# Score pairs behind the values in a fused decoder kernel's attention

## The chip, the cores and the metric

The kernel runs on one core of one Trainium2 chip. The metric is the device time of one execution in microseconds (us). Each core has five engines with their own instruction streams: TensorE (PE, with its weight loads as PEld), VectorE (DVE), ScalarE (ACT), GpSimd (POOL) and SyncE (SP, which issues the transfers here). They meet only through semaphores.

## The reference, cut to what matters

One input of 2048 tokens by 128 channels passes six layers. The fifth, attention with 16 heads of 64 channels, is the one that matters here:

```python
xn = rms_norm(x, gamma)
qkv = xn @ w_qkv                     # 16 heads, 64 channels each
sim = einsum('bhid,bhjd->bhij', q * 64 ** -0.5, k)
attn = softmax(sim, axis=-1)
out = einsum('bhij,bhjd->bhid', attn, v)
x = x + out.reshape(b, n, 1024) @ w_out
```

A softmax needs the largest score of every query first. Before attention come a mixture of experts, a recurrent layer, a second mixture and a gated layer; after it a last gated layer. Those are not touched.

## The kernel before, in words

**Tiles.** Activations lie transposed, 128 channels by 2048 tokens. A head is worked through in four chunks c of 512 queries (`NC`, `CH`), and a chunk in eight groups g of two key tiles of 128 (`GROUPS`). I write (c,g). Precision comes from splitting: a value is an upper part (rounded) plus a lower part (the rest), and products are summed over the parts that matter.

**What TensorE does in a group** (`main_chunk`, line 941, in the tensor block), all matmuls with 512 columns:

- `scores_t` (line 879, matmuls at L890 and L891): the transposed scores of this head, two key tiles, four matmuls into two of four PSUM banks. It waits for ScalarE to be done with the group two before.
- `score_pair` (line 859, L868): two matmuls for the *next* head, 128 queries by 1024 keys, into banks 4 and 5. Only the maxima are taken from them. There is one such buffer, so each pair waits on `s_max` for the maximum of the pair before. `PAIRS_OF_MAXIMA` says how many pairs a group has: none in (0,0), two in (0,7), one in each other: 32 a head.
- `values` (line 894, L905 and L908): the probabilities of the group three before (`PV_LAG`) by V, four matmuls. It waits for the upper part from ScalarE and the lower part from POOL.
- then what the plan `SPARE` places into the one spare bank (6 or 7): turned maxima (L876), column sums (`column_sums`, L917), output product of an earlier chunk (`project_out`, L924), V of the next pair of heads (`project_v`, L854 to L856), Q and K two heads ahead (`project_qk`, L713 to L715). In chunk 3 the plan has the projection n=0 in (3,3), column sums in (3,4), projection n=1 in (3,5), output in (3,6), projection n=2 in (3,7). Before each of these, `evicted` (line 926) makes TensorE wait until the one before has been taken out of the bank. For a projection that is until both ScalarE (`hi_done`) and VectorE (`lo_done`) are done.

**What VectorE does in a group** (`main_chunk`, line 1626), in this order: a piece of the row sums (`whole_sum` of the chunk before, L1588, in groups 0 to 3; `first_half_sum`, L1574, in groups 4 to 7), then, where due, `low_qk` (L1564, lower half of a projection, in (3,4) and (3,6) by `LOW_QK`, and in (0,0) and (0,2) of the next head), `add_out` (L1612, adds an output product to x: in group 0, and in (3,7)), `invert` (L1608), `maxima_end` (L1600), and last `maximum` (line 1591, L1594) for each pair of the group.

ScalarE makes two exponentials of a group's scores (L1267, L1270), and evicts. POOL makes the lower part of the probabilities (`low_part`, L609), scales outputs (L632) and, once a head, makes V's lower part (L615). All these orders are written out by hand and are the same in all heads, but for the first, the last, and that heads 14 and 15 project no Q and K two heads ahead.

Of the kernel before, what the change touches and what calls it, by code (L numbers as in the profile page):

```python
# [38 lines left out]
PAIRS_OF_MAXIMA = ((0, 1, 1, 1, 1, 1, 1, 2), (1,) * 8, (1,) * 8, (1,) * 8)  # L39
# [47 lines left out]
def macaron_kernel(nc, a, out, g_scratch, l_scratch, r_scratch):  # L87
    ctx = ExitStack()
    with ctx:
# [165 lines left out]
        def chunk(c):  # L255
            return ds(c * CH, CH)
# [5 lines left out]
        def spare_bank(c):  # L262

            return 6 + (c + 1) % 2

        def chunk_of(head, c):

            return NC * head + c

        def before(head, c, by):  # L270

            c -= by
            while c < 0:
                head, c = head - 1, c + NC
            return head, c

        def exists(head):

            return not isinstance(head, int) or head >= 0

        def wait_hi_moved(eng, head, par, n):

            eng.wait_ge(hi_moved[par], 16 * MOVES_HI * (2 * (head - par) + n + 1))

        def wait_lo_moved(eng, head, par, n):

            eng.wait_ge(lo_moved[par][n % 2], 16 * MOVES_LO * (head - par + n // 2 + 1))
# [5 lines left out]
        def spare_plan(head, c, par, project, has_next):  # L293

            plan = []
            for at, kind, n in SPARE[c]:
                if kind == "v" and not (project and par == 0):
                    continue
                if kind == "qk" and not project:
                    continue  # L300
                if kind == "turn" and n == 0 and not has_next:
                    continue
                if kind == "turn" and n == 1 and isinstance(head, int) and head == 0:
                    continue
                if kind == "sums" and not exists(before(head, c, 1)[0]):
                    continue
                if kind == "out" and not exists(before(head, c, 2)[0]):
                    continue
                plan.append((at, kind, n))
            return plan  # L310
# [369 lines left out]
        def _(pe):  # L680
# [178 lines left out]
            def score_pair(head, par, q):  # L859

                it, half = PAIR_AT[q]
                if q == PAIR_AT.index((0, half)):
                    wait_hi_moved(pe, head, par, 2 * half + 1)
                    for n in (2 * half, 2 * half + 1):
                        wait_lo_moved(pe, head, par, n)
                pe.wait_ge(s_max, PRIME + MAXIMA * head + q)
                for b in range(2):
                    last = mm(ps[:, 4 + b, :], qa[par][:, it * 128:it * 128 + 128], ka[par][:, chunk(2 * half + b)],  # L868
                              start=True, stop=True)
                last.then_inc(s_ps, 1)  # L870
# [8 lines left out]
            def scores_t(head, par, c, g):  # L879

                n = GROUPS * chunk_of(head, c) + g
                if g == 0 and c < 2:
                    pe.wait_ge(m_loaded, 16 * (2 * head + c + 1))
                if not (isinstance(n, int) and n < 2):
                    pe.wait_ge(raw_done, n - 1)
                    pe.wait_ge(ph_done, n - 1)
                for j in range(2):
                    jt = 2 * g + j
                    st = ps[:, 2 * (g % 2) + j, :]
                    mm(st, ka[par][:, jt * 128:jt * 128 + 128], qa[par][:, ds(c * CH, CH)], start=True, stop=False)  # L890
                    last = mm(st, kb[par][:, jt * 128:jt * 128 + 128], qb[par][:, ds(c * CH, CH)], start=False, stop=True)  # L891
                last.then_inc(st_ps, 1)
# [48 lines left out]
            def main_chunk(pair, par, c, has_next, project, late_project):  # L941
                head = 2 * pair + par
                last = isinstance(head, int) and head == HEADS - 1
                plan = [] if last else spare_plan(head, c, par, project, has_next)
                pairs = iter(range(sum(map(sum, PAIRS_OF_MAXIMA[:c])), MAXIMA))
                for g in range(GROUPS):
                    scores_t(head, par, c, g)
                    maxima = PAIRS_OF_MAXIMA[c][g] if has_next else 0
                    if maxima > 0:
                        score_pair(head + 1, 1 - par, next(pairs))  # L950
                    if g == PV_LAG:

                        if c > 0:
                            then = (head, pair, c - 1)
                            previous = [] if last else spare_plan(head, c - 1, par, project, has_next)
                        else:
                            then = (head - 1, pair + par - 1, NC - 1)
                            previous = spare_plan(head - 1, NC - 1, 1 - par, late_project, True) if exists(head - 1) else []
                            if late_project:
                                previous.append((0, "qk", 3))  # L960
                        for _, kind, n in previous[-1:]:
                            evicted(*then, kind, n)
                        if last and c > 0:
                            pe.wait_ge(end_r, c)
                    if g >= PV_LAG:
                        values(head, par, c, g - PV_LAG)
                    elif exists(before(head, c, 1)[0]):
                        earlier = before(head, c, 1)
                        values(earlier[0], par if c > 0 else 1 - par, earlier[1], GROUPS - PV_LAG + g)
                    if maxima > 1:  # L970
                        score_pair(head + 1, 1 - par, next(pairs))
                    if c == 0 and g == LATE_QK and late_project:
                        spare = spare_bank(NC - 1)
                        evicted(head - 1, pair + par - 1, NC - 1, "qk", 2)
                        project_qk(1 - par, NC - 1, spare)
                    spare = spare_bank(c)
                    for i, (at, kind, n) in enumerate(plan):
                        if at != g:
                            continue
                        if i == 0:  # L980
                            if exists(before(head, c, 1)[0]):
                                pe.wait_ge(o_done, chunk_of(head, c))
                        else:
                            evicted(head, pair, c, plan[i - 1][1], plan[i - 1][2])
                        scaled, summed = before(head, c, 2), before(head, c, 1)
                        if kind == "turn":
                            turn_maxima(head + 1 - n, par if n == 1 else 1 - par, n, spare)
                        elif kind == "sums":
                            column_sums(*summed, spare)
                        elif kind == "out":  # L990
                            project_out(scaled[0], par if c >= 2 else 1 - par, scaled[1], spare)
                        elif kind == "v":
                            if n == 0:
                                pe.wait_ge(vw_lo, pair + 2)
                            project_v(n, spare)
                        elif kind == "qk":
                            if n == 0:
                                pe.wait_ge(qkw_lo, head + 3)
                            project_qk(par, n, spare)
                    if last:  # L1000
                        if (c, g) == (0, END_TURN):
                            pe.wait_ge(o_done, chunk_of(head, c))
                            turn_maxima(head, par, 1, spare)
                        if (c, g) == (0, END_LATE_OUT):
                            project_out(HEADS - 2, 0, 2, 4)
                        if g == END_SUMS:
                            if c == 0:
                                pe.wait_ge(mt_done, 2 * HEADS)
                            else:
                                pe.wait_ge(o_done, chunk_of(head, c))  # L1010
                            end_sums(*before(head, c, 1), spare)
                        if g == END_OUT and c > 0:
                            end_out(c - 1)
# [730 lines left out]
```

## Time and profile before

| | us |
|---|---|
| median of 3 runs | 2112.22 |
| lowest and highest | 2109.78, 2115.67 |
| the profiled execution | 2112.44 |
| its span in the profile | 2110.4 |
| the window of attention's groups in it | 599 to 2050 |

The profile is of one execution. A page gives shares of busy time by engine; the timeline gives starts and durations, `x2` being two neighbouring instructions of a line merged into one row. The ends of matmuls are modelled, so neighbouring ones overlap in it, and their distance is to be read from start to start. Releasers of waits are inferred.

### The profile page before, as it was taken

The numbers are of one execution on the slowest core, as the hardware profiler recorded it, in microseconds if no ns is written. First come the engines' busy times: TensorE is split into PE (matmuls) and PEld (weight loads), VectorE is DVE, ScalarE is ACT, GpSimd is POOL, SyncE is SP. The second block draws the span as 40 slices with busy tenths as digits, with TensorE's granted clock in tenths as the row PEclk, the third lists the DMA queues.
The fourth block names the chain that finished last, engine by engine and source line by source line (L and its number), as shares of the span: only waits on it lengthen the run. The fifth ranks groups of instructions, "written<-read, shape, count | busy, mean of one in ns | idle before, by whom it ended". The sixth has DMA issues, their size and how long they took to land. (4 is left out here: it accounts for less than half of the span.)

```text
span 2110.4 us, 25547 instructions
## 1 busy us (share of the span) xinstructions
PE 1995.6 (95%) x8290; PEld 1421.2 (67%) x8290; DVE 1751.8 (83%) x1959; ACT 1460.5 (69%) x1800; POOL 1553.2 (74%) x772
## 2 busy tenths in 40 slices
PE   7999999997689999999999999999999999999977
PEld 5777777775557676766766766676666667666645
DVE  5787777665678998899899899889989989989865
ACT  4555455444257887788788788878878878878854
POOL 4343233232058999999899989989989998999983
PEclk9999999998789999999999999999999999999997
DMA  7201101210501230303223031222303122130000
GB/s 186 51 31 41 41 19 23 64 32 2 124 0 29 56 75 18 71 20 71 43 50 71 14 71 31 60 51 43 71 14 76 31 55 58 32 71 17 6 0 20
DMA packets 78942, 96.77 MB, mean 46 GB/s; under 512 B 32055, under 2 KB 35559, under 8 KB 78431
## 3 DMA queue, kind: packets, MB, share of 16 engines
q1 hardware_dynamic: 78814, 95.15, 20.1%
q8 instruction: 70, 1.15, 0.2%
q14 instruction: 58, 0.48, 0.1%
HBM read 43.19 MB, written 1.42 MB: 21 GB/s over the span
## 5 line engine op out<-in xcount | busy, mean ns | idle before, releaser
L609 POOL TENSOR_TENSOR p_l<-p_raw,p_h 128x1024 fp32r<-128x1024 f32 x512 | 1241.3, 2456 | 133.4 <-ACT p_h L1270 118.2
L1267 ACT ACTIVATE p_raw<-ps 128x1024 f32<-128x1024 f32 x512 | 566.3, 1106 | 230.0 <-PE ps L891 229.0
L1594 DVE TENSOR_REDUCE m_part<-ps 128x1 f32<-128x1024 f32 x480 | 584.4, 1218 | 126.1 <-PE ps L868 125.0
L1270 ACT ACTIVATE p_h<-ps 128x1024 fp32r<-128x1024 f32 x512 | 522.4, 1020 | 0.0
L890 PE MATMUL ps<-qa,ka 128*128 128x512 f32 x1024 | 444.1, 434 | 2.0 <-ACT m_t L1238 2.0
L905 PE MATMUL ps<-p_h,v_hl 128*128 128x512 f32 x1024 | 402.9, 393 | 11.4 <-POOL p_l L609 11.4
L891 PE MATMUL ps<-qb,kb 65*128 65x512 f32 x1024 | 408.6, 399 | 0.0
L1588 DVE TENSOR_REDUCE l_sum<-p_raw 128x128 f32<-128x1280 f32 x256 | 376.7, 1476 | 1.4 <-ACT p_raw L1267 1.3
L868 PE MATMUL ps<-ka,qa 128*128 128x512 f32 x960 | 314.7, 409 | 13.1 <-DVE m_part L1594 12.7
L908 PE MATMUL ps<-p_l,v_hl 128*64 128x512 f32 x1024 | 320.8, 394 | 0.0
L1574 DVE TENSOR_REDUCE p_raw<-p_raw 128x128 f32<-128x1024 f32 x256 | 308.6, 1208 | 6.3 <-ACT p_raw L1267 6.3
L549 POOL TENSOR_TENSOR x<-x,y_gated 128x512 f32<-128x512 f32 x64 | 89.2, 1394 | 265.6 <-DVE y_gated L1462 265.5
L890 PEld LDWEIGHTS ps<-qa,ka 128*128 128x128 f32 x1024 | 194.4, 190 | 113.0 <-issue 71.7
L1453 DVE SCALAR_TENSOR_TENSOR h_l<-ps,h_h 128x512 fp32r<-128x512 f32 x256 | 175.9, 688 | 111.7 <-ACT h_h L1173 109.7
L1173 ACT ACTIVATE h_h<-ps 128x512 fp32r<-128x512 f32 x256 | 150.7, 596 | 169.2 <-PE ps L715 168.4
L905 PEld LDWEIGHTS ps<-p_h,v_hl 128*128 128x128 f32 x1024 | 192.9, 188 | 92.3 <-issue 11.5
L868 PEld LDWEIGHTS ps<-ka,qa 128*128 128x128 f32 x960 | 172.2, 190 | 91.1 <-DVE m_part L1594 58.0
L891 PEld LDWEIGHTS ps<-qb,kb 65*128 65x128 f32 x1024 | 194.6, 190 | 52.7 <-issue 15.8
L908 PEld LDWEIGHTS ps<-p_l,v_hl 128*64 128x64 f32 x1024 | 138.0, 135 | 70.3 <-issue 0.2
L713 PE MATMUL ps<-x_h,w_l 128*128 128x512 f32 x256 | 117.7, 460 | 5.7 <-DVE h_l L1453 3.7
L715 PE MATMUL ps<-x_l,w_h 128*128 128x512 f32 x256 | 102.1, 399 | 0.0
L714 PE MATMUL ps<-x_h,w_h 128*128 128x512 f32 x256 | 101.9, 398 | 0.0
(206 smaller groups left out, 2389.4 us busy)
## 6 DMA issues: line engine op xcount, KB each, us to landing
g_bc<-g_scratch SPq DMA_DIRECT2D x64, 256.0 KB, 5.1
xn<-r_scratch SPq DMA_DIRECT2D x59, 256.0 KB, 4.0
qa<-qk_hi SPq DMA_DIRECT2D x112, 128.0 KB, 2.4
ka<-qk_hi SPq DMA_DIRECT2D x56, 128.0 KB, 2.4
kb<-qk_hi SPq DMA_DIRECT2D x56, 128.0 KB, 2.4
ka<-xn SPq DMA_DIRECT2D x28, 128.0 KB, 2.3
qb<-xn SPq DMA_DIRECT2D x28, 128.0 KB, 2.4
ka<-qk_low SPq DMA_DIRECT2D x28, 128.0 KB, 2.7
```

Source lines behind the costliest of these rows:

```text
L609: nc.gpsimd.tensor_tensor(p_l[:, g % 4, :, :], slots(g), p_h[:, g % 4, :, :].bitcast(fp32), ALU.subtract).then_inc(pl_done, 1)
L868: last = mm(ps[:, 4 + b, :], qa[par][:, it * 128:it * 128 + 128], ka[par][:, chunk(2 * half + b)], start=True, stop=True)
L890: mm(st, ka[par][:, jt * 128:jt * 128 + 128], qa[par][:, ds(c * CH, CH)], start=True, stop=False)
L891: last = mm(st, kb[par][:, jt * 128:jt * 128 + 128], qb[par][:, ds(c * CH, CH)], start=False, stop=True)
L905: return mm(ps[:, bank, :], v_hl[:, par, 2 * g + j, :], p_h[:, g % 4, j, :], start=start, stop=stop)
L908: return mm(ps[0:DH, bank, :], v_hl[:, par, 2 * g + j, 0:DH], p_l[:, g % 4, j, :], start=False, stop=False)
L1267: af(slots(g), s_t, ACT.Exp).then_inc(raw_done, 1)
L1270: af(p_h[:, g % 4, :, :], s_t, ACT.Exp).then_inc(ph_done, 1)
L1453: stt(h_l[:, t % 4, :], ps[:, t % 4, :], 0.0, h_h[:, t % 4, :].bitcast(fp32), ALU.max, ALU.subtract).then_inc(h_done, 1)
L1574: nc.vector.tensor_reduce(p_raw[:, ACC, cols, 0], p_raw[:, 0:ACC, cols, :].rearrange("p g n b -> p n g b"), AX.XY, ALU.add).then_inc(half_ ...
L1588: nc.vector.tensor_reduce(l_sum[:, cols], p_raw[:, ACC:GROUPS + 1, cols, :].rearrange("p g n b -> p n g b"), AX.XY, ALU.add).then_inc(all_ ...
L1594: nc.vector.tensor_reduce(m_part[:, it, half:half + 1], ps[:, 4:6, :].rearrange("p b n -> p (b n)"), AX.X, ALU.max).then_inc(s_max, 1)
```

## The change

In `main_chunk` of the tensor block, `score_pair` of a group is issued after `values`, and not between `scores_t` and `values`. In (0,7), which has two pairs, the first also moves behind the values, next to the second. The wait that a pair needs moves with it. The plan's extra matmuls still come last in the group.

```diff
                 for g in range(GROUPS):
                     scores_t(head, par, c, g)
-                    maxima = PAIRS_OF_MAXIMA[c][g] if has_next else 0
-                    if maxima > 0:
-                        score_pair(head + 1, 1 - par, next(pairs))
                     if g == PV_LAG:
...
                     elif exists(before(head, c, 1)[0]):
                         earlier = before(head, c, 1)
                         values(earlier[0], par if c > 0 else 1 - par, earlier[1], GROUPS - PV_LAG + g)
-                    if maxima > 1:
+                    for _ in range(PAIRS_OF_MAXIMA[c][g] if has_next else 0):
                         score_pair(head + 1, 1 - par, next(pairs))
                     if c == 0 and g == LATE_QK and late_project:
```

## Rows read from the trace of the kernel before

**Rows 1.** The page, part 1: busy us, share of the span and instructions by engine

```profile
PE 1995.6 (95%) x8290; PEld 1421.2 (67%) x8290; DVE 1751.8 (83%) x1959; ACT 1460.5 (69%) x1800; POOL 1553.2 (74%) x772
```

**Rows 2.** Windows view, 1300 to 1400: length, busy us by engine, PEclk, DMA, GB/s

```profile
1300.00:1400.00 100.00, 99.21 (x427) 70.07 (x426) 89.64 (x85) 79.39 (x91) 93.08 (x43) 1.00 0.19 44
```

**Rows 3.** TensorE's waits, 600 to 2050: us in total, times, longest us

```profile
PE ps L868 <- DVE m_part L1594: 12.7, 31, 1.1
PE ps L905 <- POOL p_l L609: 11.4, 14, 2.0
```

**Rows 4.** Timeline of TensorE, head 9, (3,4) to (3,6): start us, us, instructions

```profile
1497.49 0.63 PE L868 MATMUL ps<-ka,qa 128*128 128x512 f32 x2
...
1498.97 1.02 PE L917 MATMUL ps<-l_sum,inv_c 128*1 128x512 f32 x2
...
1500.97 0.63 PE L868 MATMUL ps<-ka,qa 128*128 128x512 f32 x2
...
1504.47 0.39 PE L905 MATMUL ps<-p_h,v_hl 128*128 128x512 f32 x1
...
1505.40 1.02 PE L924 MATMUL ps<-xn,w_o 128*128 128x512 f32 x2
```

**Rows 5.** Timeline of TensorE, head 9, (0,7) to (1,3)

```profile
1439.77 0.63 PE L868 MATMUL ps<-ka,qa 128*128 128x512 f32 x2
...
1441.72 0.73 PE L868 MATMUL ps<-ka,qa 128*128 128x512 f32 x2 [0.40 <-DVE m_part L1594]
1442.28 1.02 PE L924 MATMUL ps<-xn,w_o 128*128 128x512 f32 x2
...
1444.07 0.63 PE L868 MATMUL ps<-ka,qa 128*128 128x512 f32 x2
...
1446.95 0.72 PE L868 MATMUL ps<-ka,qa 128*128 128x512 f32 x2 [0.39 <-DVE m_part L1594]
...
1449.47 0.73 PE L868 MATMUL ps<-ka,qa 128*128 128x512 f32 x2
...
1451.99 0.74 PE L868 MATMUL ps<-ka,qa 128*128 128x512 f32 x2
```

**Rows 6.** Timeline of VectorE, head 9, (0,7) to (1,2)

```profile
1440.44 1.23 DVE L1594 TENSOR_REDUCE m_part<-ps 128x1 f32<-128x1024 f32 x1
1442.48 1.23 DVE L1594 TENSOR_REDUCE m_part<-ps 128x1 f32<-128x1024 f32 x1 [0.82 <-PE ps L868]
...
1445.70 1.19 DVE L1594 TENSOR_REDUCE m_part<-ps 128x1 f32<-128x1024 f32 x1
...
1448.20 1.21 DVE L1594 TENSOR_REDUCE m_part<-ps 128x1 f32<-128x1024 f32 x1
...
1450.73 1.21 DVE L1594 TENSOR_REDUCE m_part<-ps 128x1 f32<-128x1024 f32 x1
```

**Rows 7.** Timeline of VectorE, head 9, (3,4) to (3,7)

```profile
1497.87 0.74 DVE L1564 SCALAR_TENSOR_TENSOR xn<-ps,qk_scale,qk_hi 128x512 fp32r<-128x512 f32 x1
...
1501.64 1.23 DVE L1594 TENSOR_REDUCE m_part<-ps 128x1 f32<-128x1024 f32 x1 [0.77 <-PE ps L868]
1502.78 1.21 DVE L1574 TENSOR_REDUCE p_raw<-p_raw 128x128 f32<-128x1024 f32 x1
1503.99 0.75 DVE L1564 SCALAR_TENSOR_TENSOR qk_low<-ps,qk_scale,qk_hi 128x512 fp32r<-128x512 f32 x1
...
1506.94 0.68 DVE L1612 SCALAR_TENSOR_TENSOR x<-ps,x 128x512 f32<-128x512 f32 x1
```

**Rows 8.** Groups of instructions, VectorE, 600 to 2050: count, busy us, mean ns, idle before

```profile
L1564 DVE SCALAR_TENSOR_TENSOR qk_low<-ps,qk_scale,qk_hi 128x512 fp32r<-128x512 f32 x28 | 20.9, 747 | 1.9 <-ACT qk_hi L1217 1.9
L1564 DVE SCALAR_TENSOR_TENSOR xn<-ps,qk_scale,qk_hi 128x512 fp32r<-128x512 f32 x28 | 20.7, 741 | 0.0
```

**Rows 9.** Timeline of POOL and of TensorE, head 8, (0,4) to (0,7)

```profile
1343.42 7.20 POOL L609 TENSOR_TENSOR p_l<-p_raw,p_h 128x1024 fp32r<-128x1024 f32 x3
...
1346.52 0.39 PE L905 MATMUL ps<-p_h,v_hl 128*128 128x512 f32 x1
```

## The prediction, made before the changed kernel ran

> **What bounds the kernel now.** I read four views, in this order. The page's busy shares [rows 1] show TensorE at 95%, but its matmul ends are modelled, so that share proves nothing by itself. The windows view of a stretch in the middle of attention [rows 2] shows POOL 93% and VectorE 90% beside it: three engines close together, so the order of waits decides, not one total. The waits of TensorE over all of attention [rows 3] are small: 12.7 us in 31 waits for `maximum`, 11.4 us in 14 for POOL. Only waits long enough to show behind the modelled ends are in there, so I went on to starts in the timeline. Four value matmuls take 1504.47 to 1505.40, 0.93 us or 0.233 each [rows 4]. A group of ten (scores S four, values V four, pair M two) therefore takes 2.33 us, of which a pair is 0.47. TensorE starts a matmul each 0.233 us nearly without holes, at a granted clock of 1.00, the 2.4 GHz level [rows 2]. **TensorE bounds attention**, and what counts is every place where it is made to wait. I write (c,g) for chunk and group, and use head 9, which has the usual pattern.
>
> The Trainium skill (Perfetto Trace Analysis, Identifying the Most-Contended Engine) says that matmul busy share is no measure and judges TensorE by its weight loads instead. By that POOL would be the bound; this is the second rival below.
>
> **What the change moves.** Nothing is added or removed: 480 pairs, each now 0.93 us later after the scores of its own group, and the values 0.47 us earlier. No DMA and no other engine's program is touched. The extra matmuls of a group (turned maxima, column sums, output, projections) stay where they were, ten matmuls behind the group's start. `maximum` reads what the pair wrote, and VectorE runs in order, so **all that VectorE does behind a maximum moves 0.93 us later against TensorE's groups**. That is the step that matters. It is worked through below for each thing that waits.
>
> *The pair's own wait.* Each pair waits for the maximum before it. From pair to pair there is still one whole group, in both orders, and VectorE has moved as far as the pairs have. So these waits stay, at 0.
>
> *Group (0,7), with two pairs.* There M V M becomes V M M. Now the first pair starts at 1439.77, its maximum 0.67 later at 1440.44, and the second pair at 1441.72 [rows 5, 6], where without a wait it would start at 1439.77+0.47+0.93 = 1441.17: 0.55 of wait. Afterwards: first pair 1440.70, maximum 1441.37 to 1442.60, second pair 1442.66 by the 0.06 that now lie between a maximum's end (1445.70+1.19 = 1446.89) and the next pair (1446.95). That is 0.94 more wait. It comes back: before, (1,1) waits 0.55 (1444.07+0.47+0.93+0.93 = 1446.40 unhindered, 1446.95 in fact), and (1,2) and (1,3) wait too [rows 5]. Afterwards the pair of (1,1) comes 0.94+0.93 later, at 1448.27, and its maximum is ready at 1446.89+0.94 = 1447.83. The next pairs come at 1450.60 against 1448.20+0.94+1.21 = 1450.35, and 1452.93 against 1452.88+0.06 = 1452.94. In that last group, (1,3), the pair stands 0.95 later than the 1451.99 of before, and 0.93 of that is its new place. VectorE's unbroken chain from (0,7) to (1,3) sets the time in both orders. **Net 0.02 us a head, taken as 0**.
>
> *The lower halves of Q and K in chunk 3.* `low_qk` for (3,4) follows the maximum and the sum of the group before it on VectorE, and ends at 1497.87+0.74 = 1498.61 [rows 7]. `evicted` makes the column sums in (3,4) wait for it. They start at 1498.97 [rows 4], so the spare is about 0.3. Moved by 0.93, the lower half ends at 1499.54, and TensorE goes on at 1499.60: 0.63 late. A wait also costs the preloading of weights: two matmuls span 0.72 after a wait against 0.63 without, by the busy columns at 1446.95 and 1444.07 [rows 5]. I take 0.09 for it: **0.72 us**. Behind it on TensorE stands everything, the next scores first, and ScalarE, VectorE and POOL wait for those; VectorE gets 0.72 us nearer, but it is not what TensorE waits for in (3,5). The bounds are 0 (if the spare were larger) and 0.93 (if there were none).
>
> The Trainium skill (TensorE: Matmul & The Clock Gate, Step-by-step: what each phase is for) has the next weights pulled ahead of running matmuls. Taken without limit the 0.09 would not be paid, and the whole sum below would be about 2.5 us smaller. The two spans of rows 5 show that the load does not hide behind a late wait.
>
> *The second lower half, (3,6).* With TensorE 0.72 late, the maximum of (3,5) goes from 1501.64 to 1501.64+0.72+0.93 = 1503.29, the sum follows at 1504.43, `low_qk` 1.13 later at 1505.56 (a sum's 1.21 less the 0.08 by which neighbours overlap), with 0.75 to 1506.31 [rows 7]. Before it had idled for its input until 1503.99; that cover is used up. The output matmul of (3,6), due at 1505.40+0.72 = 1506.12 [rows 4], starts at 1506.37: 0.25 and again 0.09, **0.34 us**.
>
> *The add in (3,7).* The maximum of (3,6) follows at 1504.00 (the pair: 1504.47 less 0.47) +0.93+0.72+0.67 = 1506.32, the sum at 1507.46, `add_out` at 1508.59 and, with 0.68 [rows 7], ends at 1509.27. The third projection, due at 1505.40+0.86+2.33 = 1508.59 now (0.86 is the output product in (0,7), 1442.28 to 1443.14, the 1444.07 less 0.93 [rows 5]), comes at 1508.59+1.06 = 1509.65. Spare 0.3: **0**.
>
> This happens where Q and K are projected two heads ahead, heads 0 to 13. The two groups of `low_qk` count 28 and 28, four a head [rows 8]. **14 x 1.06 = 14.8 us**.
>
> *Values earlier.* They need POOL's lower part. In even heads POOL also scales V's; in head 8 the lower part for (0,7) is ready at 1343.42+2.45 = 1345.87, by the third of 7.20, and the values start at 1346.52: 0.65 spare, and 0.18 after the change [rows 9]. I take 0 here, and up to 0.1 in 8 heads. If POOL were late there, each such head would lose up to 0.47: 4 us at most.
>
> *New neighbours.* Scores to values, values to pair and pair to scores may each have another interval than 0.233. No undisturbed row shows all three. By the 0.23 to 0.24 between starts in rows 4 and 5 the bound is 0.01 a group either way, 5 us over 480; I take 0, in the middle.
>
> **Sum.** 14.8 us, all on TensorE's path. The profiled execution took 2112.44 us (span 2110.4), 0.2 above the median of 2112.22, so the sum goes to **2127.2 us**, +0.7%.
>
> **Rivals.**
> - *The pair's waits vanish* (faster). If a maximum gained the 0.93 us of the values as extra time, the four waits of head 9, 0.64+0.64+0.2+0.2 with their loads, would go in 15 heads: 25 us, 2087 us. For it: rows 3 name this wait as TensorE's largest. Against it: the distance from pair to pair is the same, and in (0,7) it shrinks. It decides if VectorE's start, not its chain, sets these waits, that is if maxima start 0.67 after their pair; in (1,1) to (1,3) they do not [rows 5, 6]. Chance 0.09.
> - *POOL is the bound, or the lower halves come early enough* (no change). Then a microsecond of TensorE's is swallowed elsewhere: 2113 us. For it: POOL's 93%. Against it: values seldom wait for POOL, 14 times in 512 groups [rows 3]. Or VectorE does not drift by the whole 0.93; under 0.3 of drift nothing happens at (3,4). Chance 0.18.
> - *The 0.94 of (0,7) is not given back* (slower still): 0.94 x 15 = 14 on top, 2141 us. It decides if something else than the maximum chain holds (1,1) to (1,3), such as ScalarE waiting for the row sums, which also end 0.93 later. Chance 0.13.
> - Forecast, 0.60.
>
> **Range and chances.** A measurement of this kernel can tell about 0.3%, 6 us, from no change. The range goes from the no-change case, 2113, to 2140: the forecast with 5 for neighbours, 4 for POOL and some of the last rival. Faster 0.09, same 0.18, slower 0.73.
>
> **What would show it.** In the changed profile TensorE's column sums of (3,4) should start 0.7 us later against their group's start, right after a `low_qk` on VectorE, and the output of (3,6) 0.3 later. Groups (3,4) and (3,6) grow from 3.4 and 2.8 us, heads 0 to 13 grow by 1.1, heads 14 and 15 by nothing. Second pair of (0,7): 1.5 us of wait, and none in (1,1) and (1,2). I am wrong if the lower halves do not move against TensorE, if heads grow anywhere else, or if head 14 grows as the others do.

## The result, and the profile after

The changed kernel takes 2126.14 us (median of 5 runs, 2125.05 to 2131.76), the kernel before 2112.22 (5 runs). The ratio is 1.0078 with an interval of 1.0066 to 1.0089: **slower by 0.8%**. The forecast was 2127.2 us. The profiled execution took 2125.89 us, with a span of 2123.9 against 2110.4, so 13.5 us more. TensorE's granted clock is 1.00, the 2.4 GHz level, from 600 to 2000 in both traces, so the clock is not the cause.

First the page, part 1, against [rows 1], and the windows view of the same stretch, 1300 to 1400, against [rows 2]:

```profile
PE 1993.6 (94%) x8290; PEld 1420.3 (67%) x8290; DVE 1749.8 (82%) x1959; ACT 1459.8 (69%) x1800; POOL 1554.9 (73%) x772
```

```profile
1300.00:1400.00 100.00, 97.96 (x415) 68.45 (x414) 90.12 (x85) 79.66 (x91) 94.70 (x44) 1.00 0.22 45
```

No engine works more. TensorE's busy share in the stretch goes from 99.21 to 97.96: there are holes now that the modelled ends don't cover. Who makes them is in TensorE's waits, 600 to 2060, against [rows 3]:

```profile
PE ps L868 <- DVE m_part L1591: 19.7, 15, 1.3
PE ps L905 <- POOL p_l L609: 10.0, 14, 1.5
PE ps L917 <- issue: 8.4, 14, 0.6
```

The third row is new: 14 waits of the column sums (L917), one in each of heads 0 to 13, 0.6 us each. The profile names nobody for it ("issue"). The first row tells of the second pair of (0,7): 15 waits, one a head, 1.3 us each, where 31 shorter ones stood before. This view alone would make the maxima the culprit. They are not, as the group lengths show. Its second row misleads too. In both traces nearly all of these 14 waits for POOL are of head 15, which has no pairs: 13 before, 11 after. The shorter waits for POOL that the change makes in odd heads are not in it but for one, in head 13; they show in starts alone.

A group's length is the distance from its first score matmul to the next group's. I took it in the trace for the groups of all heads and subtracted the kernel before's. The median over heads of one parity is good to about 0.02 us:

| group | growth in even heads, us | growth in odd heads, us |
|---|---|---|
| (0,7) | +0.97 | +0.91 |
| (1,1), (1,2), (1,3) | -0.65, -0.21, -0.07 | -0.65, -0.21, -0.07 |
| (1,4), (1,7) | +0.01, -0.01 | **+0.16, +0.24** |
| (3,4) | **+0.66** | **+0.67** |
| (3,6) | **+0.36** | **+0.36** |
| each other group | about 0.02 at most | about 0.02 at most |

From the first group's start to the last one's the growth is 16.4 us. Heads 0 to 9 and 11 to 13 grew by 1.0 to 1.7 us each, head 10 by 0.7, and head 15, which has no pairs, by 0.1. Head 14 shrank by 1.4: in the execution before, its (0,3) had waited 1.3 us for a lower half whose upper half came late, behind a transfer. ScalarE's wait for that transfer, just there, was 1.7 us; its longest of the kind in the execution after is 0.8. In heads 6 and 10 (0,7) grew by 1.38 and 1.27, not by the usual 0.97: its values waited 0.40 and 0.30 us for POOL. The 2.9 us between 16.4 and 13.5 lie outside attention, where the code is the same; over the twelve traces that part takes 666.8 to 671.7 us.

The timeline of TensorE in head 9, (3,4) to (3,7), answers to [rows 4]:

```profile
1509.62 0.62 PE L868 MATMUL ps<-ka,qa 128*128 128x512 f32 x2
...
1510.85 1.02 PE L917 MATMUL ps<-l_sum,inv_c 128*1 128x512 f32 x2 [0.60 <-issue]
...
1516.79 0.62 PE L868 MATMUL ps<-ka,qa 128*128 128x512 f32 x2
1517.54 1.10 PE L924 MATMUL ps<-xn,w_o 128*128 128x512 f32 x2
```

and VectorE's in the same stretch to [rows 7]:

```profile
1510.00 0.74 DVE L1561 SCALAR_TENSOR_TENSOR xn<-ps,qk_scale,qk_hi 128x512 fp32r<-128x512 f32 x1
...
1516.70 0.74 DVE L1561 SCALAR_TENSOR_TENSOR qk_low<-ps,qk_scale,qk_hi 128x512 fp32r<-128x512 f32 x1
```

The lower half ends at 1510.00+0.74 = 1510.74 and the column sums start at 1510.85. The second ends at 1516.70+0.74 = 1517.44, and the output product starts at 1517.54. Before, these matmuls started 0.36 and 0.66 us after the halves had ended [rows 4, 7]. That the waits are for the halves is inferred from this distance of 0.10 to 0.11 and from `evicted`; the experiments test it.

Group (0,7) and what follows it, TensorE in head 9, against [rows 5]:

```profile
1451.48 0.63 PE L868 MATMUL ps<-ka,qa 128*128 128x512 f32 x2
1453.42 0.74 PE L868 MATMUL ps<-ka,qa 128*128 128x512 f32 x2 [1.32 <-DVE m_part L1591]
...
1456.71 0.62 PE L868 MATMUL ps<-ka,qa 128*128 128x512 f32 x2
...
1459.04 0.63 PE L868 MATMUL ps<-ka,qa 128*128 128x512 f32 x2
...
1461.36 0.63 PE L868 MATMUL ps<-ka,qa 128*128 128x512 f32 x2
```

The second pair starts 1.94 us after the first, with nothing between but a wait. In (1,1) and (1,2) the waits of before are gone: each pair is followed by the next after 2.33 or 2.32 us.

### The profile page after: what moved, and what is told of

The parts are those of the page before. It is cut to its first block and busy times, and to the rows that moved or that the text cites. A ratio compares the mean times of both kernels' runs of the same rounds, so it can differ in the third digit from the quotient of the medians.

```text
span 2123.9 us, 25547 instructions
## 1 busy us (share of the span) xinstructions
PE 1993.6 (94%) x8290; PEld 1420.3 (67%) x8290; DVE 1749.8 (82%) x1959; ACT 1459.8 (69%) x1800; POOL 1554.9 (73%) x772
## 5 line engine op out<-in xcount | busy, mean ns | idle before, releaser
L868 PE MATMUL ps<-ka,qa 128*128 128x512 f32 x960 | 310.1, 404 | 19.7 <-DVE m_part L1591 19.7
```

## The experiments

Theory: VectorE does all that stands behind a maximum 0.93 us later, and TensorE loses what it then waits for lower halves in chunk 3. The new thing to explain was the 0.4 us of odd heads. Lengths below are medians as above, from one profiled execution each. A ratio is to the kernel before as it ran beside that experiment (medians 2111.3 us for e1 to e4, 2110.2 for e5 to e8, 2112.0 for e9 and e10), with a 95% interval.

**e1: the lower halves ahead of the row sums.** The changed kernel, with in VectorE's `main_chunk`:

```diff
                 for g in range(GROUPS):
+                    if (c, g) in LOW_QK and project:
+                        low_qk(head + 2, par, LOW_QK[c, g], spare_bank(c), qk_hi, qk_low[LOW_QK[c, g] % 2], True)
                     if g >= GROUPS // 2:
...
-                    if (c, g) in LOW_QK and project:
-                        low_qk(head + 2, par, LOW_QK[c, g], spare_bank(c), qk_hi, qk_low[LOW_QK[c, g] % 2], True)
```

> The changed kernel, with VectorE taking the lower half of the projection (low_qk) ahead of the row sums' piece in (3,4) and (3,6). My theory: the waits of the column sums in (3,4), 0.67 us, and of the output product in (3,6), 0.36 us, are waits for these halves, so both go in heads 0 to 13: 14 x 1.03 = 14.4 us off the 2126.1 of the changed kernel, 2112 us, ratio 1.000 to the kernel before. The second pair of (0,7) still waits 1.5 us and POOL still holds the values of (1,4) and (1,7) in odd heads. Rival (new neighbours of matmuls, or POOL or the maxima set the loss): 2126 us, and (3,4) and (3,6) stay as long or the time turns up in the next groups.

Measured: 2118.6 us, ratio 1.0038 (1.0017 to 1.0059). Against the changed kernel (3,4) is 0.68 us shorter and (3,6) 0.37, so both waits are gone to 0.01. But (3,7) is 0.31 longer, the heads gain 0.73 each, not 1.03, and the time misses the expected 2112. The profile of e1, VectorE and then TensorE in head 9, (3,7):

```profile
1514.75 0.68 DVE L1609 SCALAR_TENSOR_TENSOR x<-ps,x 128x512 f32<-128x512 f32 x1
```

```profile
1514.81 0.62 PE L868 MATMUL ps<-ka,qa 128*128 128x512 f32 x2
1515.48 0.50 PE L713 MATMUL ps<-x_h,qk_l 128*128 128x512 f32 x1
```

The third projection stands behind the pair and was due at 1515.28. It starts at 1515.48, when `add_out` has ended at 1515.43. In the kernel before the add ended 0.97 us ahead of this projection (1507.62, 1508.59), in the changed kernel 0.41 (1520.40, 1520.81), which is the spare of 0.3 that I had reckoned. Of the 0.41 the stall in (3,6) gave 0.36, since it stands between the pair and the projection. e1 takes it away, and VectorE gets 0.19 later against that pair: its `low_qk` now waits 0.20 for ScalarE, and all behind it follows without a gap. I had not asked what is left of the spare without the stall.

**e2: the lower halves late, with the order of before.** The kernel before, `low_qk` of chunk 3 behind the maximum:

```diff
-                    if (c, g) in LOW_QK and project:
-                        low_qk(head + 2, par, LOW_QK[c, g], spare_bank(c), qk_hi, qk_low[LOW_QK[c, g] % 2], True)
...
                     for _ in range(PAIRS_OF_MAXIMA[c][g] if has_next else 0):
                         maximum(head + 1, next(pairs))
+                    if (c, g) in LOW_QK and project:
+                        low_qk(head + 2, par, LOW_QK[c, g], spare_bank(c), qk_hi, qk_low[LOW_QK[c, g] % 2], True)
```

> The kernel before, pairs ahead of the values, but VectorE takes low_qk of (3,4) and (3,6) behind the group's maximum, about 1.1 to 1.4 us later. My theory: lateness of these halves alone slows TensorE. (3,4) grows by 1.2 us, (3,6) by 1.3, 2.5 us in each of 14 heads, 35 us: 2147 us, ratio 1.017. Rival (the order of matmuls is what costs, the halves have room or the time is made good elsewhere): 2112 to 2117 us.

Measured: 2145.2 us, ratio 1.0154 (1.0135 to 1.0172). (3,4) grew by 1.16, (3,6) by 1.33, and no other group by more than 0.03. The matmuls stood where they had always stood. So lateness of the halves is enough by itself to make TensorE lose time in just these two groups, and e1 shows that in the changed kernel the whole loss there is theirs.

**e3: in (0,7) the first pair back between scores and values.** The changed kernel, with

```diff
                     scores_t(head, par, c, g)
+                    maxima = PAIRS_OF_MAXIMA[c][g] if has_next else 0
+                    if maxima > 0 and (c, g) == (0, 7):
+                        score_pair(head + 1, 1 - par, next(pairs))
+                        maxima -= 1
...
-                    for _ in range(PAIRS_OF_MAXIMA[c][g] if has_next else 0):
+                    for _ in range(maxima):
```

> The changed kernel, but in (0,7) the first of the two pairs goes back between scores and values. My theory: the chain of maxima on VectorE from (0,7) to (1,3) sets that stretch in either order, so (0,7) gets 0.94 us shorter and (1,1) to (1,3) together 0.92 longer, 0.0 net. What does go is POOL's lateness of odd heads, (1,4) and (1,7) 0.16 and 0.24 us, since TensorE no longer makes up 0.9 us in (1,1) to (1,3): 7 x 0.4 = 2.8 us. 2123 us, ratio 1.0065. Rival (the wait of the second pair is a loss by itself and is not given back): 15 x 0.94 = 14 us off, 2112 us.

Measured: 2129.3 us, ratio 1.0086 (1.0068 to 1.0104). Theory and rival were both wrong. (0,7) is shorter by 0.12 us in even heads and 0.06 in odd ones, (1,1) to (1,3) are unchanged, and the 0.4 us of odd heads stay. TensorE in e3, the pairs of (0,6) and (0,7):

```profile
1452.26 0.63 PE L868 MATMUL ps<-ka,qa 128*128 128x512 f32 x2
1454.20 0.73 PE L868 MATMUL ps<-ka,qa 128*128 128x512 f32 x2 [0.39 <-DVE m_part L1595]
1456.46 0.73 PE L868 MATMUL ps<-ka,qa 128*128 128x512 f32 x2 [0.61 <-DVE m_part L1595]
```

I had forgotten the pair of (0,6), which now stands behind its values. From it to the moved pair only a pair and four scores are left, 1.40 us, and the maximum takes longer: the pair waits until 1454.20. Moving a pair ahead in one group takes from one distance what it gives the next. So e3 did not undo the wait; it split it. It speaks for the theory's core (the distance counts), and against my use of it.

**e4: V's split later in odd heads.** The changed kernel, with

```diff
-V_SPLIT = ((0, 3), (1, 0))
+V_SPLIT = ((0, 3), (2, 5))
```

> The changed kernel, but POOL and ScalarE make V's split for the next head in (2,5) instead of (1,0) in odd heads. My theory: the 0.16 and 0.24 us by which (1,4) and (1,7) of odd heads grew are waits of the values for POOL's lower part, which stands behind 2.43 us of V's split. Both go, 2.8 us in 7 heads, 2123.3 us, and nothing comes back in chunk 2, where POOL has 1.4 us or more in hand. Rival (these 0.4 us come from the second pair of (0,7) or from the row sums that ScalarE waits for): no change, 2126 us, and (1,4) and (1,7) stay as long.

Measured: 2126.3 us, ratio 1.0075 (1.0055 to 1.0095). In the trace (1,4) and (1,7) of odd heads are 0.16 and 0.24 us shorter, exactly what the change had put on, and no other group changed by more than 0.02. The time of the runs doesn't show 2.8 us, and 2123.3 was not reached: the interval is wider than that, 4 us each way. The 0.4 us are POOL's. Why it is late is in its timeline, in head 9, (1,0) to (1,4), of the kernel after:

```profile
1458.11 2.46 POOL L609 TENSOR_TENSOR p_l<-p_raw,p_h 128x1024 fp32r<-128x1024 f32 x1 [2.73 <-issue]
1460.53 2.41 POOL L615 TENSOR_TENSOR v_hl<-v_raw,v_hl 128x1024 fp32r<-128x1024 f32 x1
1462.90 2.45 POOL L609 TENSOR_TENSOR p_l<-p_raw,p_h 128x1024 fp32r<-128x1024 f32 x1
```

POOL can start on (1,0) only when its probabilities have come, and the second pair of (0,7) holds those back longer than before: POOL's idle time ahead of it is 2.73 us and was 1.80. From there to (1,1) it has no gap. The lower part of group (1,1) is ready at 1462.90+2.45 = 1465.35, and the values that use it, in (1,4), start at 1465.50, where they were due at 1465.22:

```profile
1465.50 0.48 PE L905 MATMUL ps<-p_h,v_hl 128*128 128x512 f32 x1
```

Before, the same lower part ended at 1451.14+2.50 = 1453.64, and its values started at 1455.10, 1.46 us later:

```profile
1451.14 2.50 POOL L609 TENSOR_TENSOR p_l<-p_raw,p_h 128x1024 fp32r<-128x1024 f32 x1
```

```profile
1455.10 0.39 PE L905 MATMUL ps<-p_h,v_hl 128*128 128x512 f32 x1
```

(1,4) grew by less than the new wait, since the wait of its pair, 0.19 us before, is gone in return. Two things took 1.40 of the 1.46 us: the values stand 0.47 us earlier in the group, and TensorE made good 0.93 us in (1,1) to (1,3) where POOL did not. How much each counts is worked out here; no run separates them.

**e5: three fixes.** e1 and e4 together, and `add_out` of (3,7) also ahead of the row sums:

```diff
+                    if (c, g) == (NC - 1, LAST_ADD) and not last:
+                        add_out(head, c - 2, spare_bank(c))
                     if (c, g) in LOW_QK and project:
...
-                    if (c, g) == (NC - 1, LAST_ADD) and not last:
-                        add_out(head, c - 2, spare_bank(c))
```

> The changed kernel with pairs behind the values, and three things of other engines moved to fit: low_qk of (3,4) and (3,6) and the add_out of (3,7) ahead of VectorE's row sums, and V's split of odd heads in (2,5). My theory: every microsecond that the change cost is a wait for one of these, so (3,4), (3,6), (3,7) and odd (1,4), (1,7) are as short as in the kernel before, heads 0 to 13 fall by 1.03 us each and odd ones by 0.4 more, and 2126.1 becomes 2126.1 - 14.4 - 2.8 = 2109, ratio between 0.998 and 1.001. The 0.31 us that (3,7) took in e1 must go. Rival: the order S V M costs by itself, and 5 us or more are left.

Measured: 2114.3 us, ratio 1.0015 (0.9995 to 1.0035). The 2109 us expected were not reached, and the times alone don't put the rival out: the interval goes up to 1.0035, 7 us. The groups do. In sum attention's are 0.07 us longer than in the kernel before. All heads but 0, 6, 10 and 14 are within 0.07 us of it; those four, with +0.2, +0.7, +0.3 and -1.4 us, differ between single executions. In heads 6 and 10 the values of (0,7) wait 0.69 and 0.73 us for POOL. (3,4), (3,6), (3,7) and odd (1,4), (1,7) are within 0.02 of it. (0,7) has its +0.96 and (1,1) to (1,3) their -0.92, which cancel. The rival is out: scores, values, pair is not a dearer order.

**e6: one pair in each group, in the kernel before.**

```diff
-PAIRS_OF_MAXIMA = ((0, 1, 1, 1, 1, 1, 1, 2), (1,) * 8, (1,) * 8, (1,) * 8)
+PAIRS_OF_MAXIMA = ((1,) * 8,) * 4
```

> The kernel before, pairs ahead of the values, with one pair in each group: (0,0) gets one and (0,7) has one, not two. My theory: what costs is a short distance from pair to pair, and the maximum between. (0,7) loses 0.47 us of matmuls and 0.64 of wait, (1,1) to (1,3) together about 1.0 of wait, (0,0) grows by 0.47, and (0,3) and (0,4) by about 0.5, since VectorE has a maximum more there. Net 1.5 to 1.6 less with the matmuls equal, minus 0.5: 1.0 us in each of 15 heads, 2097 us, ratio 0.993. Rival (VectorE's whole work sets the time from (0,0) to (1,3), wherever the pairs stand): 2112 us.

Measured: 2100.9 us, ratio 0.9963 (0.9948 to 0.9977). (0,0) +0.45, (0,3) +0.35, (0,4) +0.13, (0,7) -1.12, (1,1) -0.65, (1,2) -0.21: as reckoned, 1.1 us in odd heads. Even heads got 0.3, for (1,3) grew by 0.74 there: the wait named below. So the 2097 us expected were missed by 4.

**e7: the three fixes and one pair in each group**, behind the values.

> The three fixes of e5 and one pair in each group, pairs behind the values. My theory: (0,7) loses the 1.58 us of the second pair's wait and 0.47 of matmuls, (0,0) grows by 0.47, (0,3) and (0,4) by 0.5: 1.1 us in 15 heads below e5, 16 us, 2094 us, ratio 0.991. Rival (order S M V is the better one where distances are even too): above e6 by 3 us or more.

Measured: 2102.6 us, ratio 0.9961 (0.9948 to 0.9974). The expected 2094 us were missed by 8.6. Against e5 (0,7) is 2.1 us shorter, but (1,3) of even heads is 0.78 longer, and all groups together gain 12.2 us where 16 were expected. The rival that needs 3 us more than e6 is out: the groups are 0.6 us shorter than in e6. Of its waits of TensorE, 590 to 2050, one row is new in size:

```profile
PE ps L854 <- POOL wv_hl L625: 5.4, 7, 1.6
```

These are seven waits of V's projection for the lower half of V's weights, which POOL makes in (1,1). TensorE had gained 1 us before that place, and POOL, which works through 14.53 us of lower parts in a row up to there, had not:

```profile
1339.60 14.53 POOL L609 TENSOR_TENSOR p_l<-p_raw,p_h 128x1024 fp32r<-128x1024 f32 x6
```

**e8: chunk 3 alone back to the order of before** (the edit of e3 with `c == 3` as its condition), one execution.

> The changed kernel with the pairs of chunk 3 alone back between scores and values. From (2,7) to (3,0) the distance between pairs is then 0.93 us shorter. My theory: that costs as much once, where VectorE's chain of maxima has no room: against the changed kernel (3,1) +0.6, (3,2) +0.2, (3,3) 0, and (3,4) -0.67, (3,6) -0.36, net about -0.2 us in heads 0 to 13 and +0.8 in head 14. From (3,7) to (0,1) the distance is longer and nothing changes. Rival (waits hang on where a pair stands in its group, not on its distance to the one before): chunk 3 as in the kernel before, 1.0 us less a head and nothing in (3,1).

Measured: 2129.0 us in the one execution, which by itself decides nothing; head 0 alone is 3.6 us longer in it than in the changed kernel. Against the changed kernel by groups: (3,1) +0.65, (3,2) +0.20, (3,3) +0.07, (3,4) -0.67, (3,6) -0.36, head 14 +0.9. Each term came out as reckoned from the chain of maxima, and the rival, with nothing in (3,1), is out. A distance shortened once costs what VectorE has no room for.

**e9 and e10: a version that beats both.** e6 and e7, each with POOL's lower halves of the weights in (0,7):

```diff
-                        if (c, g) == (1, 1) and project:
+                        if (c, g) == (0, GROUPS - 1) and project:
```

> e6 (one pair in each group, pairs ahead of the values as in the kernel before), and POOL makes the lower halves of the next weights in (0,7) instead of (1,1). In e6 (1,3) of even heads grew by 0.74 us since the V projection waits for POOL's L625. My theory: it goes, 5 us in 7 heads, to about 2096 us, ratio 0.994. Rival (POOL is full there, so the values of even (0,7) or odd (1,4) wait instead): as e6, 0.996.

> e7 (three fixes, one pair in each group, pairs behind the values), and POOL's lower halves of the weights in (0,7). My theory: (1,3) of even heads falls by 0.78 us, 5 us less than e7, and the two orders are the same within 2 us when nothing waits for the later maximum. Rival (pairs behind the values are the better or worse order in themselves): 4 us or more between this run and e9.

Measured: e9 2095.3 us, ratio 0.9925 (0.9906 to 0.9945); e10 2096.9 us, ratio 0.9931 (0.9911 to 0.9950). Even and odd heads now both gain 1.1 us, 18.3 us over attention's groups in e9. Between e9 and e10 the groups differ by 0.06 us in sum; the two intervals are 4 us wide each way and could not show this. Both orders of pair and values are equally good where nothing waits for the later maximum, and e9, with fewer edits, is the one to keep.

## Why the prediction was right

The number fits better than its parts. Point by point:

- *The lower halves in chunk 3.* Forecast 0.72 and 0.34 us, measured 0.67 and 0.36, in 14 heads: 14.4 us where 14.8 was forecast. e1 takes just these away, and e2 makes them without the change. The 0.09 for the weights not preloaded was taken from pairs and was wrong for the column sums. In the trace before they start 0.32 us after the matmul ahead of them in each of 59 cases, without any wait, where other matmuls start 0.23 after. Their weight load starts only with them (both at 1498.97 in head 9). So they paid the 0.09 already, and the wait adds itself alone: 0.67, put at 0.63. The output product in (3,6) starts 0.29 late and its group grows by 0.36, so there 0.07 comes on top.
- *Group (0,7) and its return.* Forecast +0.94 and back; measured +0.91 to +0.97, and -0.93 in (1,1) to (1,3). The chain of maxima sets this stretch. The rival that it is not given back is out. So is the one that all waits vanish: TensorE's waits for maxima, now 19.7 us against 12.7 in that view, are fewer and longer.
- *The pair's own wait, elsewhere.* Forecast 0, measured within 0.02.
- *Values earlier.* Here the step failed. I looked at POOL in even heads alone, at (0,7), and counted 0.47 us of earliness. In odd heads the values of (1,4) and (1,7) meet POOL behind V's split, and to the 0.47 comes the 0.93 that TensorE makes good just ahead. That is 0.4 us in 7 heads, 2.8 us, where I had 0. e4 shows that it is POOL behind V's split. In the even heads the 0.18 us left at (0,7) held in all but heads 6 and 10, which lost 0.7 together. By the prediction's own sign, "if heads grow anywhere else", this part of it was wrong.
- *New neighbours.* Forecast 0 within 5 us. Undisturbed groups have the same length within 0.02, and e5 and e10 show nothing for the order. The bound was too wide.
- *The add in (3,7).* Forecast 0, and that held in the changed kernel; e1 shows that it held only by the stall in (3,6).
- *The sum.* 14.4 and 2.8 make 17.2. One long wait of head 14 in the execution before takes 1.4 off, and 0.6 comes from single heads, 6 and 10 among them, which makes 16.4, and the rest of the kernel was 2.9 us quicker in that execution. That the forecast lay 1.1 us off the median is in part these cancelling.
- *POOL as the bound* is out. It has 94.70 of 100 us busy in the stretch, and a delay of TensorE of 1 us a head came through whole. One argument that I had against it was weak: the 14 waits for POOL in rows 3 are 13 of head 15 and one of head 0, and a view of waits shows none of the short ones that count here.

What stays open: what makes heads 0, 6 and 10 differ from execution to execution. In 6 and 10 the last step is POOL, late for the values of (0,7) in the traces of the changed kernel and of e5 and not in those of e1, e3 and e4; what makes POOL late there is not shown.

## What to carry to other kernels

When an operation moves later on one engine, follow what stands *behind its consumer* on the consumer's in-order engine, not the consumer alone: the pair's maximum had room, the halves 2 us behind it had 0.3. When a stall of TensorE goes or a delay is made good, ask at once which engine TensorE meets in the next microseconds, for that engine has not been sped up: this made (1,4) here, (3,7) in e1 and (1,3) in e6 and e7. And with one buffer between producer and consumer, the evenness of their distances is what counts: one pair in each group, with one of POOL's operations moved to suit, won 17 us, while the order within the group was worth nothing.

## What the runs showed that I had not expected

A wait on a semaphore that another engine's operation gives was put down to nobody (`L917 <- issue`), while it made 9.3 of the 16.4 us. The wait with the largest total in TensorE's list, for the maxima, grew from 12.7 to 19.7 us, and that growth cost nothing net; two pairs in (0,7) and none in (0,0) cost 1.1 us a head in either order, as the odd heads of e6 and e7 show. And a wait of this kind can be read to about 0.02 us from group lengths, where the runs' own interval was 2 to 4 us wide on each side: medians over 7 heads of one profiled execution settled what the timed runs could not, as in e4.
